# Four chunks of 12, 9, 5 and 2 pairs in place of five of 8, 8, 6, 4 and 2 in an attention and mixture-of-experts kernel

## The reference

```
x = x + attention(layernorm(x), ctx) @ Wproj + bproj      # 16 heads of 64, 128 keys of 192 channels
t = layernorm(x)
probs = softmax(t @ gate_w.T)                             # 8 experts
top2_w, top2_idx = top_k(probs, 2)
mixed = sum over the two of top2_w * silu(t @ expert_w[e].T + expert_b[e])
x = x + mixed @ combine_w.T
```

## The kernel before

| chunk | pairs | blocks | `turn_block` in slots | pairs' places in `plan.mix` |
|---|---|---|---|---|
| 0 | 0 to 7 | 39 | 78 to 116 | 127 to 153 |
| 1 | 8 to 15 | 39 | 142 to 180 | 191 to 217 |
| 2 | 16 to 21 | 31 | 190 to 220 | 231 to 249 |
| 3 | 22 to 25 | 23 | 222 to 244 | 255 to 261 |
| 4 | 26 and 27 | 15 | 245 to 259 | 266 and 268 |

## Time and profile before

### The profile page before, as it was taken

How to read it: one execution, slowest core, us unless ns; L and a number is a source line. 1 busy time by engine, 2 the same in 40 slices (tenths; PEclk the granted TensorE clock), 3 DMA queues, 4 the chain that set the end, 5 groups by cost and what they waited for, 6 DMA issues and landing times.

```text
span 1635.4 us, 39352 instructions
## 1 busy us (share of the span) xinstructions
PE 1537.0 (94%) x11891; PEld 1470.2 (90%) x11891; DVE 1264.0 (77%) x3135; ACT 1062.0 (65%) x2890; POOL 879.9 (54%) x1185
## 2 busy tenths in 40 slices
PE   4999999998999999999999999999999999999787
PEld 4899999998999999998999999899998998999675
DVE  5788888777888888877877888877778787776566
ACT  4766666665666766675767667666766666666433
POOL 4655555555545555576655545575656465644410
PEclk9999999999999999999999999999999999999999
DMA  6633333333577777344677667467777776877722
GB/s 226 203 85 91 92 91 92 91 91 95 173 216 223 223 217 210 101 123 128 201 224 227 204 213 217 135 188 226 230 227 211 220 229 198 248 218 216 273 64 78
DMA packets 179131, 286.99 MB, mean 175 GB/s; under 512 B 23575, under 2 KB 113900, under 8 KB 178668
## 3 DMA queue, kind: packets, MB, share of 16 engines
q1 hardware_dynamic: 168172, 255.11, 52.7%
q0 software_dynamic: 10752, 29.37, 5.8%
HBM read 155.66 MB, written 61.62 MB: 133 GB/s over the span
## 4 chain that ended last, share of the span: by engine, by line
PE 73%; DVE 10%; issue 6%; ACT 5%; POOL 4%; DMA 1%; SPq 0%; ACTq 0%; DVEq 0%; POOLq 0%
PE gen_ps L566 21%; PE qk_ps L566 15%; PE o_ps L566 9%; PE proj_ps L566 9%; PE s_ps L566 8%; PE pT_ps L607 6%; ACT stage L801 2%; PE gen_ps L690 1%; PE gen_ps L657 1%; PE gen_ps L665 1%; DMA k_s<-qk_s 1%; DVE sums L1015 1%; ACT v_s_hi L801 1%; POOL sorted_x L1328 1%; POOL stage L1309 1%
## 5 line engine op out<-in xcount | busy, mean ns | idle before, releaser
L828 ACT ACTIVATE stage<-s_ps,neg_max 128x128 f32<-128x128 f32 x1024 | 292.8, 371 | 105.8 <-DVE neg_max L1008 95.7
L1318 POOL CAST o_s_hi<-stage 128x256 fp32r<-128x256 f32 x256 | 102.2, 399 | 477.0 <-ACT stage L801 471.8
L1309 POOL TENSOR_TENSOR stage<-stage,inv_sums 128x512 f32<-128x512 f32 x256 | 266.8, 1042 | 15.9 <-DVE inv_sums L1017 15.9
L801 ACT CAST pT_s_hi<-pT_ps 128x512 fp32r<-128x512 f32 x256 | 150.9, 589 | 150.9 <-PE pT_ps L607 141.8
L566 PE MATMUL s_ps<-k_s,qk_s 128*128 128x256 f32 x1536 | 226.6, 283 | 4.1 <-DMA k_s<-qk_s 3.2
L1015 DVE TENSOR_REDUCE sums<-stage 128x4 f32<-128x512 f32 x256 | 172.9, 676 | 66.5 <-ACT stage L828 56.7
L960 DVE TENSOR_TENSOR pT_s_lo<-pT_ps,pT_s_hi 128x512 fp32r<-128x512 f32 x256 | 172.8, 675 | 56.0 <-ACT pT_s_hi L801 50.3
L960 DVE TENSOR_TENSOR qk_s<-qk_ps,qk_s 128x512 fp32r<-128x512 f32 x256 | 175.8, 687 | 41.8 <-ACT qk_s L801 39.0
L566 PEld LDWEIGHTS s_ps<-k_s,qk_s 128*128 128x128 f32 x1536 | 201.4, 191 | 4.9 <-DMA k_s<-qk_s 3.9
L1320 POOL TENSOR_TENSOR o_s_lo<-stage,o_s_hi 128x256 fp32r<-128x256 f32 x256 | 188.0, 734 | 21.1
L801 ACT CAST v_s_hi<-gen_ps 128x512 fp32r<-128x512 f32 x129 | 75.7, 587 | 177.2 <-PE gen_ps L566 173.3
(11 more groups left out here) (358 smaller groups left out, 4706.1 us busy)
## 6 DMA issues: line engine op xcount, KB each, us to landing
w_block<-expert_table SPq DMA_DIRECT2D x147, 512.0 KB
k_s<-qk_s SPq DMA_DIRECT2D x512, 128.0 KB
stage<-sorted_x SPq DMA_DIRECT2D x147, 128.0 KB
sorted_y<-stage SPq DMA_DIRECT2D x147, 128.0 KB
x_raw<-in_x SPq DMA_DIRECT2D x32, 256.0 KB
c_raw<-in_ctxT SPq DMA_DIRECT2D x32, 256.0 KB, 3.3
stage<-in_x SPq DMA_DIRECT2D x32, 256.0 KB
x_kept<-x SPq DMA_DIRECT2D x32, 256.0 KB
```

The lines of the kernel that those rows point to most:

```text
L801: last = act.copy(to, of)
L828: last = act.activation(probs[p % 2][:, k, :], s_ps[:, k * P:(k + 1) * P], ACT.Exp, bias=neg_max[p % 2][:, k:k + 1])
L1309: pool.tensor_tensor(probs[b][:, :, :], probs[b][:, :, :], inv_sums[b][:, :].unsqueeze(2).broadcast_to([P, 4, P]), ALU.mult).then_inc(prob ...
L1318: pool.tensor_copy(hi[:, :, :], o_full).then_inc(o_hi, 1)
```

## The change

One line is changed. The 28 sparse pairs are cut into four chunks instead of five.

```diff
-CHUNKS = (8, 8, 6, 4, 2)
+CHUNKS = (12, 9, 5, 2)
 SPARSE = sum(CHUNKS)
```

## The result

| | before | four chunks of 12, 9, 5, 2 |
|---|---|---|
| median | 1632.61 us (1629.04 to 1637.51, 4 runs) | 1675.39 us (1671.58 to 1678.79, 4 runs) |
| ratio | | 1.0264, interval 1.0241 to 1.0287 |
| profiled execution, span | 1637.44, 1635.4 | 1671.58, 1669.5 |
| attention ends (slot 256 begins) | 1521.8 | 1486.5 |
| last dense product ends | 1613.1 | 1623.1 |

The change costs 42.8 us in the medians. The profiled execution of the changed kernel is the fastest of its four, that of before is among its slowest, so the two profiles differ by only 34.1 us. The mean granted clock of the four was 0.982 in the profiled one and 0.975, 0.977 and 0.979 in the others, so part of the missing 8.7 us may be clock; no run separates it.

The account below looks back on a forecast made before the run. TensorE sets the pace in attention; in the tail it waits for banks VectorE drains only after its dense debt. The terms -27.3 + 46.9 + 19.8 = +39.4 us gave 1670 us, range 1650 to 1683.

Parts of the forecast that it names:

- Part 1, attention: Iterations 9 to 31: fewer blocks and pairs and one chunk end less make attention 27.3 us shorter.
- The bound of 3 us for pairs at other positions: Iterations 29 to 31: pairs standing at other positions could cost between 0 and 3 us more.
- Part 2, slots 256 to 267: Tail slots: blocks now reach slot 266, each such slot has the bank wait; 46.9 us longer.
- The `weigh` put at nothing: Tail slots: weigh, 1.7 us, is covered by the wait on TensorE's queue and costs nothing.
- Part 3, behind the last dense product: After the dense work: eight pairs left instead of four, pair 26 awaiting the last block; 19.8 us longer.
- The clock that stays up: Rival: the clock does not fall after each stand, seven tail slots lose 1.7 us each; 1658 us, chance 0.17.
- The blocks that hide: Rival: slots 261 to 267 gain only seven blocks' work, at most 1.2 us each; about 1631 us, chance 0.07.
- idle time that takes the moved work: Rival: new pairs' turns fall into the tail's stands, adding only TensorE's own work; 1623 us, chance 0.08.
- The last chunk that comes still later: Rival: gathers landing in 5 us or moved pairs' extra attention costs (3 us) add up; 1680 us, chance 0.13.

Follow-up runs that it names:

- Experiment 1: VectorE does expert_out and combined ahead of a slot's dense work: in the changed kernel 1622.94 us (0.9963 of before), in the kernel before 1614.75 us (0.9919).
- experiment 4: Kernel before with chunks of 12, 8, 5 and 3, last block in slot 259: 1631.78 us; with expert_out and combined ahead of dense work too: 1614.15 us.
- Experiment 3: Changed kernel with idle TensorE products in slots 260 to 266: 1664.03 us; with more behind the last dense product too: 1660.3 us.
- a_fill: Changed kernel with ten idle TensorE products in front of the waiting job of slots 260 to 266: 1664.03 us, ratio to before 1.0211.
- the two fills: Changed kernel with idle products in slots 260 to 266, and in front of pair 26's turn and each combine at the end: 1660.3 us, ratio to before 1.0189.

## Why the prediction was right, point by point

- **Part 1, attention.** Forecast -27.3 us, measured 1095.3 - 1126.8 = -31.5 us for iterations 9 to 31. Right in kind and nearly in size; the excess is mostly a chunk end at which the clock did not fall, and over all profiles of the two lists it is 2.7 us, not 4.2. The bound of 3 us for pairs at other positions was not needed as a whole: iteration 29 took 56.4 where 55.4 was forecast.
- **Part 2, slots 256 to 267.** Forecast +46.9, measured 136.6 - 91.3 = +45.3 (the forecast put the end of the last dense product before at 1613.2, the table here at 1613.1). Eleven of the twelve slots lie within 1.1 us of their term; slot 258 was 10.4 instead of 12.1, as its clock did not fall. Slot 265 took 13.4 instead of 12.3, with a mean clock of 0.75. Eleven stands released by line 1031 stood where I had expected the ten of slots 257 to 266 and one more wait in 267; I had said 3 to 4 us for each, and four of the ten, in the even slots 258, 262, 264 and 266, lasted 2.85 to 2.97. The `weigh` put at nothing released no stand in these slots. Experiment 1 shows the mechanism by taking it away, and experiment 4 shows that it hangs on where the last block lies, not on four chunks.
- **Part 3, behind the last dense product.** Forecast +19.8, measured 46.4 - 22.3 = +24.1. Store to gather took 2.4 us (2.5 taken), the stand in front of pair 26 3.96 us (4 taken). The turn of pair 27 began 20.1 us behind the last dense product, where 19.9 was forecast. The term that was mis-sized is what follows it: 22.1 us forecast, 1669.5 - 1643.2 = 26.3 measured. I counted pair 27 at 4.1 us and the dense pairs at 3.6, and with the clock at 1.2 GHz pair 27 took 6.2 and pair 28 5.3. Experiment 3 gives 3.4 to 4.3 us for the clock. That the steps before came out so closely is partly luck, as two errors cancel: the last block was stored at 2.9 us instead of 3.9, and the landing of a gather took more than the 2.5 that I had borrowed from a store, 1636.05 - 1632.68 = 3.4 us from the fourth issue to the start of `weigh`.
- **The rivals.** The clock that stays up did not hold: nine of the slots 257 to 266 had a mean of 0.75 to 0.87, only slot 258 did not (nor did 267), and `a_fill` shows 9.9 us for slots 260 to 266 with the clock held in six of them, some 1.6 each, where I had taken 1.7. The blocks that hide, and idle time that takes the moved work, are refuted by lengths: the slots alone grew by 45 us, where the first needed 8, and the second a whole tail that grows by less than 22. The last chunk that comes still later is what was left over, 4 us of it.
- **The sum.** -31.5 + 45.3 + 24.1 = +37.9, and 3.8 less for the start makes the 34.1 between the two profiles; +39.4 was forecast. In the medians the change costs 42.8 us; the profiled execution of the changed kernel was the fastest of four.

## What to carry to other kernels

A plan that packs work later to save a fixed cost should be priced where the work lands, not where it leaves: here 27 to 32 us came back in attention and 69 went into a tail of other rules. Where several buffers turn in a fixed order, read which engine frees them and what it does first; moving two steps ahead of a block of other work took 16 us out of the old plan and 52 out of the new one, where neither other list of chunks made the old plan faster. After it the list of 12, 8, 5 and 3 was equal to the old one, and that of 12, 9, 5 and 2 still 8 us behind.

## What the runs showed of the hardware

TensorE's clock fell after most of its stands. In nine of the eleven tail slots with a stand the mean granted clock was 0.75 to 0.87; in slots 258 and 267, with stands of 2.86 and 2.81 us, it was 1.00, while slot 266 had 0.85 behind one of 2.85. Filling 2.3 us of the stand in seven slots with useless products held the clock in six of them and made this stretch 9.9 us shorter. How long a low clock lasts was not the same twice: behind the stand of 3.96 us in front of pair 26 it was 0.50 for 17.1 us, behind the same stand of `a_fill` (4.28 us) for about 12.3. In both TensorE then stood 1.55 us in each pair, while the clock was low and after it had come back, so these short stands alone do not hold it down. The Trainium skill, "TensorE: Matmul & The Clock Gate", Part 1, gives the penalty of a ramp, for a model, as less than 1% of a typical kernel's span; the two fills together took 15 us, 0.9%, out of this one (12 us by the ratios). For the tail of 183 us it is 7 to 8%.
